# Five stages of a transformer block in one block of engine programs, with the last sequence of one stage and the first of the next taking turns

## The reference, cut to what matters

```python
x = layernorm(x + attn(x, w_qkv, b_qkv, w_out, b_out))          # stage 1
def layer(x):                                                   # twice
    h = shift_token(x)            # the second half of the features comes from the token before
    q, k, v = split(h @ wqkv)     # 8 heads of width 64
    q, k = l2norm(q) * q_scale, l2norm(k) * k_scale
    q, k = rotary_xpos(q, k)
    o = local_attention(q, k, v)  # windows of 128, softmax over this and the last window
    x = x + o @ wo                                              # stages 2 and 4
    h = layernorm(shift_token(x)) * ln_g + ln_b
    a, g = split(h @ w1 + b1)     # 2 x 682
    return x + (a * gelu(g)) @ w2 + b2                          # stages 3 and 5
out = layernorm(x + layer(layer(x)))
```

## Time and profile before

| | |
|---|---|
| device time, three executions | 1912.76, 1910.35, 1907.33 us; median 1910.35 |
| profiled execution | span 1913.5 us; no device time beside the span is given |
| TensorE busy | 1775.1 us, 93% |
| VectorE, ScalarE, GpSimd busy | 60%, 52%, 45% |
| mean granted clock of TensorE | 0.937 of full |
| stage 1 loop ends, stage 2 loop begins | 461.9, 570.5 us |
| stage 2 loop ends, stage 3 loop begins | 954.4, 1018.3 us |
| stage 3 loop ends, stage 4 loop begins | 1187.5, 1262.9 us |
| stage 4 loop ends, stage 5 loop begins | 1645.9, 1710.5 us |

### The profile page before, as it was taken

One profiled execution on the slowest core, in us unless ns is written; L12 is line 12 of the kernel. 1 busy time (PEld: TensorE's weight loads), 2 busy tenths in 40 slices (PEclk: granted clock), 3 DMA queues, 4 the chain that ended last, 5 costly groups with the idle time before them and its releaser, 6 DMA issues. The chain is left out here.

```text
span 1913.5 us, 42806 instructions
## 1 busy us (share of the span) xinstructions
PE 1775.1 (93%) x14072; PEld 1346.1 (70%) x14072; DVE 1143.7 (60%) x2863; ACT 986.1 (52%) x1898; POOL 859.2 (45%) x890
## 2 busy tenths in 40 slices
PE   5999999999679999999979999599999999889997
PEld 3666665665357777777758888467777777678886
DVE  5667776667367766766633333576666776435554
ACT  2666556655336555555544444345555655534443
POOL 3333333432236655555633333445556656325444
PEclk7899888898689999999988999899999999979999
DMA  4344244344000100010021223101010000212221
GB/s 141 121 131 122 87 128 128 116 126 127 24 25 9 33 33 33 33 33 22 2 88 57 65 65 110 46 12 34 33 33 0 33 33 22 79 56 77 88 82 50
DMA packets 105656, 121.29 MB, mean 63 GB/s; under 512 B 23386, under 2 KB 78340, under 8 KB 105604
## 3 DMA queue, kind: packets, MB, share of 16 engines
q1 hardware_dynamic: 99412, 98.08, 16.8%
q0 software_dynamic: 6192, 22.55, 3.4%
HBM read 82.55 MB, written 37.77 MB: 63 GB/s over the span
## 5 line engine op out<-in xcount | busy, mean ns | idle before, releaser
L461 DVE TENSOR_REDUCE a_negm<-a_x 128x2 f32<-128x256 f32 (+3 forms) x256 | 201.3, 815 | 120.6 <-PE a_x L609 118.5
L421 ACT ACTIVATE a_PT<-a_c 128x384 f32<-128x384 f32 (+1 forms) x384 | 185.4, 524 | 137.9 <-PE a_c L648 72.5
L888 POOL TENSOR_TENSOR work<-work 128x512 f32<-128x512 f32 x128 | 164.5, 1286 | 152.7 <-DVE work L1038 151.6
L1056 DVE CUSTOM_DVE_ANT_0 l_x<-l_x,window 128x256 f32<-128x256 f32 (+1 forms) x512 | 184.0, 420 | 31.8 <-PE l_x L1155 31.7
L1578 DVE SCALAR_TENSOR_TENSOR m_hid<-m_a,mw_b,m_gate 128x512 f32<-128x512 f32 x96 | 71.9, 749 | 197.5 <-ACT m_gate L1513 168.9
L1470 POOL TENSOR_TENSOR m_hid_lo<-m_hid,m_hid_hi 128x512 fp32r<-128x512 f32 x80 | 102.8, 1294 | 180.6 <-ACT m_hid_hi L1524 180.5
L1089 PE MATMUL l_f<-w_hi,tails 128*128 128x512 f32 x384 | 168.4, 438 | 15.5 <-DVE work L1038 12.4
L971 ACT ACTIVATE l_PT<-l_c 128x512 f32<-128x512 f32 (+1 forms) x256 | 125.3, 542 | 87.8 <-PE l_c L1195 84.3
L1090 PE MATMUL l_f<-w_hi,tails 128*128 128x512 f32 x384 | 155.0, 404 | 0.0
L1091 PE MATMUL l_f<-w_lo,tails 128*128 128x512 f32 x384 | 154.4, 402 | 0.0
L902 POOL TENSOR_TENSOR l_PS<-l_PT 128x768 f32<-128x768 f32 x64 | 119.7, 1870 | 58.7 <-ACT l_PT L971 58.7
(11 more groups left out here) (240 smaller groups left out, 5096.3 us busy)
## 6 DMA issues: line engine op xcount, KB each, us to landing
a_Q<-qk_parts SPq DMA_DIRECT2D x192, 64.0 KB, 2.1
a_K<-qk_parts SPq DMA_DIRECT2D x192, 64.0 KB, 2.1
qk_parts<-a_qk_hi SPq DMA_DIRECT2D x32, 256.0 KB, 2.1
qk_parts<-a_qk_lo SPq DMA_DIRECT2D x32, 256.0 KB, 2.1
xin<-after_attn SPq DMA_DIRECT2D x32, 256.0 KB, 3.1
m_xr<-after_attn SPq DMA_DIRECT2D x16, 512.0 KB, 3.9
after_attn<-rows_out POOLq DMA_DIRECT2D x14, 512.0 KB, 5.3
xin<-in_L_attn_x SPq DMA_DIRECT2D x8, 512.0 KB, 3.5
```

What stands on the lines that cost most here:

```text
L421: nc.scalar.activation(PT[:, p // PG % 2, 2 * (p % PG) + hh, QOFF[t]:QOFF[t] + nq], SC[hh][:, 0:nq], ACT.Exp, scale=AD ** -0.5).then_inc(e ...
L461: dve.tensor_reduce(negm[:, q, 2 * p:2 * p + 2], MX[i % 2][:, :, 0:nk], AX.X, ALU.max, negate=True).then_inc(max_done, 1)
L888: pool.tensor_tensor(t1[:, par, w, :], t1[:, par, w, :], t2[:, par, w, :], ALU.add)\
L1056: m = dve.tensor_tensor_reduce(out=o, in0=o, in1=mask, scale=-1.0, scalar=-NEG, op0=ALU.add, op1=ALU.min, accum_out=negm[:, q + t, p // 2, ...
```

## The change

All five stages now return a `Stage`: its steps, its front, and one function for each engine. One `nc.Block()` holds all of them, and `follow` walks through them on each engine. Between two loops stands a list `JOINS[n]`, written out by hand, in which the last sequence's steps of stage n and the front steps of stage n+1 (with a +) take turns. There is no block end between stages.

```diff
+def follow(eng, engine, stages, joins):
+    do = [stage.engines[engine](eng) for stage in stages]
+    for name, i in stages[0].opening:
+        do[0](name, i, 0)
+    for n, stage in enumerate(stages):
+        with eng.Fori(0, NB - 1) as it:
+            for step in stage.steps:
+                do[n](*step, it + (stage.base + 1) if step in stage.ahead else it + stage.base)
+        for name, i in joins[n]:
+            if name[0] == "+":
+                do[n + 1](name[1:], i, stages[n + 1].base)
+            else:
+                do[n](name, i, stage.base + NB - 1)
```

```diff
+JOINS = [
+    parse("""
+        nx:0 +rl:0 sm:27 st:8 mt:2 st:9 pv:0 st:10 sm:28 ns:0 sm:29 st:11 sm:30 st:12 ns:1 ms:2 sm:31 +edge:0 z0:0 st:13
+        xr:0 st:14 mt:3 +f_x:0 ms:3 z1:0 pv:1 +f_xe:0 st:15 st:16 +rot:0 +f_qk:0 st:17 +f_qe:0 ms:4 st:18 +f_qk:1 st:19
+        +f_qe:1 z2:0 st:20 +f_iv:0 st:21 +f_qk:2 ms:5 z0:1 st:22 +f_qe:2 z1:1 z3:0 st:23 +f_qk:3 pv:2 +f_qe:3 ms:6 z2:1
+        +f_iv:1 ms:7 z0:2 z1:2 +f_qk:4 pv:3 +f_qe:4 z0:3 z3:1 +f_qk:5 z2:2 z1:3 z3:2 z2:3 +f_qe:5 +f_iv:2 z3:3 +f_qk:6
+        nwo:0 out:0 +f_qe:6 out:1 +f_qk:7 out:2 out:3 +f_qe:7 +f_iv:3 end:0 +pick:0 +set:0 ns:2 +f_t:0 +f_te:0 +f_sm:0
+        +f_t:1 +f_te:1 +f_sm:1 +f_t:2 +f_te:2 +f_sm:2 +f_t:3 +f_te:3 +f_sm:3 +f_v:0 +f_v:1 +f_v:2 +f_mt:0 +f_v:3
+        +banks:0"""),
+    parse("""
+        nx:0 nz:0 xr:0 nw:0 st:0 sm:4 +f_n:0 st:1 ps:0 sm:5 st:2 sm:6 pv:0 +f_m:0 sm:7 sv:0 z:0 st:3 ps:1 zn:0 mt:1 +f_t:0 st:4
+        +f_te:0 pv:1 st:5 ps:2 sv:1 z:1 nm:0 +w:0 st:6 zn:1 zs:0 ns:0 pv:2 sv:2 zs:1 z:2 st:7 zn:2 pv:3 ps:3 +set:0 sv:3
+        zs:2 ns:1 z:3 zn:3 zs:3 +f_w1:0 +f_w1:1 ns:2 out:0 +f_h:0 +f_h:1 +banks:0 +nw:0"""),
+    parse("""
+        nx:0 +rl:0 w1:2 +edge:0 h:2 ns:0 w2:0 w1:3 ns:1 +f_x:0 +f_xe:0 w2:1 +rot:0 w1:4 h:3 +f_qk:0 h:4 xr:0 +f_qe:0 w1:5
+        +f_qk:1 +tab:0 +f_qe:1 w2:2 h:5 +f_iv:0 +f_qk:2 w2:3 +f_qe:2 +f_qk:3 w2:4 +f_qe:3 +f_iv:1 w2:5 +f_qk:4 nwo:0 y:0
+        +f_qe:4 fin:0 +f_qk:5 +f_qe:5 +f_iv:2 ns:2 +pick:0 +set:0 +f_qk:6 +f_qe:6 +f_qk:7 +f_qe:7 +f_iv:3 +f_t:0 +f_te:0
+        +f_sm:0 +f_t:1 +f_te:1 +f_sm:1 +f_t:2 +f_te:2 +f_sm:2 +f_t:3 +f_te:3 +f_sm:3 +f_v:0 +f_v:1 +f_v:2 +f_mt:0 +f_v:3
+        +banks:0"""),
...
+    parse("""w1:2 h:2 w2:0 w1:3 w2:1 w1:4 h:3 h:4 xr:0 w1:5 w2:2 h:5 w2:3 w2:4 w2:5 y:0 fin:0"""),
+]
```

```diff
-                def tail(name, i):
-                    if (name, i) == FIRST_OF_LAST:
...
-                        ahead.load(sp, ahead_raw, ahead_wo)
+            elif name == "nw":
+                ahead.load(sp, ahead_raw)
                 zeros.store(sp)
...
+    return Stage(STEPS, FIRST, FIRST + [("nw", 0)], 0, sync=sync, gpsimd=gpsimd, scalar=scalar, vector=vector, tensor=tensor), left
```

```diff
+    left = Left(front=(max_done, NB * MU), maxima=(max_done, NB * MU), scores=(y_done, NB * TB),
...
+            if name == "banks":
+                pe.wait_ge(*before.scores)
+            elif name == "f_x":
+                pe.wait_ge(x_in, (b - base) * 16 + 16)
+                if isinstance(b, int):
+                    pe.wait_ge(*before.front)
...
+                if isinstance(b, int):
+                    act.wait_ge(own.lo_done, KT)
...
+            elif name == "set":
+                dve.wait_ge(*before.queries)
+                dve.wait_ge(*before.values)
```

Stages of the same kind share their semaphores; in the second layer they go on counting, so sequence numbers run from `base` = 8 there:

```diff
-                        pe.wait_ge(x_in, b * 16 + 16)
+                pe.wait_ge(x_in, (b - base) * 16 + 16)
...
-                        dve.wait_ge(stored, b * 16)
+                dve.wait_ge(stored, (b - base) * 16)
...
-                    dve.wait_ge(rots_in, 96)
+            dve.wait_ge(rots_in, 96 * lay + 96)
```

2588 lines of the change are left out of this document (1306 added, 1282 removed).

## The result

| | before | changed |
|---|---|---|
| median of 4 runs, us | 1911.55 (1907.33 to 1914.36) | 1885.66 (1882.59 to 1887.20) |
| span of the profiled execution, us | 1913.5 | 1885.1 (its own time 1886.66) |

The ratio is 0.9853 with a 95% interval of 0.9837 to 0.9869: 28 us less by the ratio, 25.9 by the medians, 28.4 between the spans. I had forecast 56.7 less (1854 us). The time lies outside the forecast's own range (1838 to 1872) and 0.3 us inside the one that reaches to the rivals (1828 to 1886): half of the gain is missing.

The account below looks back on a forecast made before the run. TensorE, busy 93%, bounds the loops, so gains lie only at the four boundaries between stages. Savings 26.2 + 9.5 + 12.9 + 12.1 less 4 at the opening give 56.7 off 1910.35: 1854 us, range 1838 to 1872, with rivals 1828 to 1886.

Parts of the forecast that it names:

- Opening: First stage's start: ten more SyncE issues delay the load of sequence 1's x; 4 us lost, bounds 0 and 9.
- Third boundary: Join between second and third loop, paced by VectorE's queue: 75.4 us before, 12.9 us less.
- thin front: Last part of the front at first and third boundary (turning, maxima, values), still following the join: 18.2 us.
- First boundary: Front's projections and rotation fit beside the last sequence, lengthening it 5 us (bounds 0, 20.4): 108.6 to 82.4, 26.2 less.
- A: Each boundary's first stretch, the last sequence alone: 59.2, 46.8, 23.2 and 45.9 us before the change.
- Second and fourth boundary: Fold and turns go into TensorE's idle time beside the last sequence; 9.5 and 12.1 us less, new stall included.
- B: Each boundary's second stretch, the next stage's first-sequence front alone: 49.4, 17.1, 52.2 and 18.7 us before.
- The stall of the first iteration: Feed-forward loops' first iteration waits for h after the last store: 4 us at second boundary, 3 at fourth, bounds 0 and 9.
- The second, in-order queues turning the joins into chains: Rival for the joins: front steps wait for TensorE and block later steps; savings halve, opening costs 7: 1888 us, chance 0.16.
- The first rival, the clock: Denser joins hold TensorE at 2.4 GHz, 24 us more saved: 1830 us, chance 0.18.
- The third: Rival: second layer's loops slow down from computing wait values with an added base; 1937 us, chance 0.03.
- The fourth rival: Joins do nothing: every first iteration waits for the last store as long as the front took; 1908 us, chance 0.02.

Follow-up runs that it names:

- masks_first: Changed kernel with GpSimd's two last causal masks moved ahead of the front's additions and products in the first join; 1882.1 us, ratio 0.9821.
- joins24: Changed kernel, second and fourth join: fold, low parts, output projection before the hidden units; SyncE's wait moved, next layer's weight load late; 1858.2 us, ratio 0.9701.
- joins24_fold_early: joins24 with the fold of the norm's shift back in front of the last scores at the second and fourth boundary; 1876.9 us, ratio 0.9809.
- fold_late: Changed kernel with only the fold moved behind the last zs step, second and fourth join; 1883.9 us, ratio 0.9832.
- next_weights_late: Changed kernel with the load of the next layer's projection weights moved from the second join's end to the third join's head; 1884.0 us, ratio 0.9839.
- joins24_weights_early: joins24 with the next layer's projection weight load back between the last store and first load of h, second boundary; 1856.6 us, ratio 0.9706.

## Why the prediction was half right

**Opening: right.** 4 us forecast, 4.1 at the turn (58.83 to 62.95), 4.6 at the last sequence. TensorE turned that x at half speed after the wait (1.96 us for 8 matmuls, 1.09 in the earlier trace rows).

**Third boundary: right, by its own steps.** The first rotated turn came 44.5 us after the last sequence's start; the forecast had 1231.5 - 1187.5 = 44. VectorE's last product ended 41.1 us after the start, with 32.0 us of work and 9 idle, where I had 30.7 of work, 3 before it and 7 of bubbles. The thin front took 18.1:

```profile
1220.48 1.97 PE L1146 MATMUL d<-ident,l_qk 128*128 128x128 f32 x8 [10.15 <-POOL l_qk L908]
...
1238.61 0.60 PE L1125 MATMUL d<-ident,xin 128*128 128x128 f32 x4
```

The step that was worked out as one engine's queue, with its bubbles, held. The others were worked out as idle time against added work.

**First boundary: the mechanism was right, the lengthening too small.** "All fit, TensorE narrowly ... I take 5, nearer to the lower end" was the step that failed: A up to the first turn took 71.2 us (466.5 to 537.7) instead of 59.2 + 5, and the thin front 19.6 instead of 18.2. The 12.0 us lie inside my bounds of 0 to 20.4. The other 1.4, in the thin front, are the clock (0.71 beside 0.78) and not the order. The sum of idle time said that there is room; the orders of the in-order queues said when. `masks_first` shows 3.2 of the 7 missing us on one queue, GpSimd, in which I had looked for nothing but its sum (16.1 us into 44.1 idle; the 16.1 should be 19.4, as the 3.26 that I took off lie before 552.3). The rest I haven't allotted to single steps. The Trainium skill (TensorE: Matmul & The Clock Gate, Architectural detail) says that ScalarE, VectorE and GpSimd each take their queue strictly in order; the trace agrees, with masks whose input was there at 504.6 running at 509.15 and 512.52. I had also expected the wait for the rotated rows to halve; it stayed whole, as the rotation's last block is still last.

**Second and fourth boundary: the failed step.** "The 44 one-column matmuls ... go beside A, where TensorE has 46.8 - 32.7 = 14.1 us idle ... For the rest I take 2.5 us that do not fit." The fold didn't lie beside A but in its chain. Its 8.7 us and the 2.27 in front of it stood on TensorE ahead of scores on which the head outputs, and so everything behind, hang. (Of the 8.7, some 3.5 are the clock: at 2.4 GHz the same fold took 5.2 in `joins24`.) A came out 12.4 us longer than without its walls (57.7 against 46.8 - 1.5) and 14.5 at the fourth (58.9 against 45.9 - 1.5); I had 5.1 at each, with upper ends of 8 + 6 = 14, which the fourth passes. Without the waits for the additions (3.95 and 4.02 us) 8.4 and 10.5 remain for what I had put at 2.5. `joins24_fold_early` against `joins24` measures the fold's place at 10.2 and 8.4 us, `fold_late` against the changed kernel at 2.3 and 5.7: how much of the missing time is the fold's alone depends on the order around it, but fold, output projection, low parts and SyncE's wait together are worth 17.4 and 11.8. Over the whole second boundary, A and B, TensorE was idle for 15.0 us before and still for 9.5 in the join. The idle 14.1 us were there, but spread in gaps of 0.7 to 2.1 us and the one wait of 6 at the end; only the last can take a piece of 5 to 9 us, and the list puts the fold in front of it.

**The output addition** waited 3.24 + 0.71 us instead of 2.6. **The stall of the first iteration** was 6.4 and 2.7 where I had 4 and 3. As idle time it was right: by the windows TensorE is idle for 17.70 - 13.95 = 3.75 us and 14.00 - 11.73 = 2.27. The other 2.65 at the second boundary are the clock, which I had left out of this term: behind the wait it is at its lower level, and a 512-column matmul takes 0.63 us where it takes 0.39 before the wait; at the fourth boundary it stays at 1.00. Most of the 4 I had given to the weights' load, wrongly. At the fourth boundary, where there is no such load, the way from the store's issue to the statistics takes 8.1 us (1678.86 to 1687.00), at the second 10.2 (998.35 to 1008.52). But in `next_weights_late`, at the second boundary and without the load, it still takes 9.4 (1000.77 to 1010.18), so under 1 of these 2 us is the load's. In `joins24_weights_early` the load costs VectorE 3.1 us of waiting and TensorE nothing. What the stall hung on was how late the store left: 16 us earlier in `joins24`, and it is gone. The Trainium skill (DMA: Bandwidth & Descriptors, Queues, rings and completion order) says that descriptors are consumed in ring order on each DMA engine; these 3.1 us of waiting agree in direction, and the stall at the upper end of 9 that I drew from it didn't come.

**The bounds** of the sum don't come out of the terms as I stated them: they give savings of 2 to 90, not 16 to 100.

**The rivals.** The second, in-order queues turning the joins into chains (1888 us), had 0.16 and is what happened, though not as it was worked out: 17.8 + 0 + 12.8 + 3 for its 13 + 4 + 6 + 6, and 4.6 at the opening for its 7. That its time is only 2 us off is luck; it strikes where a long step stands in a chain, not everywhere by half. The first rival, the clock, came in part: the first boundary's clock is 0.81 where it was 0.70 and 0.77, the second's 0.88 where it was 0.89 and 0.70. The third is out: the loops of the second layer take 272.2 us for five iterations (273.3 before) and 149.6 for six (149.3). The 0.3 us an iteration by which the third stage's loop is longer are in the first layer, whose base is 0, and stay unexplained. The fourth rival holds for the second boundary alone, by accident: its gain of 6.2 went into the 6.4 of the first iteration.

## What to carry to other kernels

When two pieces of work take turns, idle time on an engine tells what could fit; the place in each in-order queue tells what will. For each inserted step ask what stands behind it on its engine, SyncE included, and put long steps into the longest wait rather than into the first gap. When a join removes the work between a store and the load that reads it back, move the store's whole chain forward: here three steps and a wait moved together (with a load whose place showed no effect) took 29 us off, where the fold alone had taken 4 off (2.3 and 5.7 by J2 and J4) and the projection alone had added 9.
